# Cross-attention with a merged FFN: two groups of probability products issued as one, the merged weights made a turn later, and a new timetable

## What is computed

```python
x = x + attention(layernorm(x), ctx)      # 16 heads of 16, softmax over 512 keys
x = x + ffn(layernorm(x), W1, b1, W2, b2) # row g has its own W1[g], W2[g]

# attention
qh = heads(q @ Wq.T + bq) / 4;  kh = heads(k @ Wk.T + bk);  vh = heads(v @ Wv.T + bv)
attn = softmax(qh @ kh.T);      out = merge(attn @ vh) @ Wo.T + bo
# ffn: no nonlinearity between the two products
h1 = x @ W1[g].T + b1[g];       h2 = h1 @ W2[g].T + b2[g]
```

## Time and profile before

| | us |
|---|---|
| median of 3 runs | 609.21 (607.52 to 611.81) |
| the profiled execution's own time | 607.91 |
| its span, first to last instruction | 606.1 |
| first `exp` | 40.2 |
| eight turns, first `exp` to the last one's end | 542.5 |
| tail behind the last `exp` | 23.3 |

### The profile page before, as it was taken

One profiled execution on the slowest core, in us unless ns is written; L12 is line 12 of the kernel. 1 busy time (PEld: TensorE's weight loads), 2 busy tenths in 40 slices (PEclk: granted clock), 3 DMA queues, 4 the chain that ended last, 5 costly groups with the idle time before them and its releaser, 6 DMA issues.

```text
span 606.1 us, 13508 instructions
## 1 busy us (share of the span) xinstructions
PE 563.9 (93%) x4353; PEld 342.9 (57%) x4353; DVE 457.4 (75%) x841; ACT 392.5 (65%) x703; POOL 273.5 (45%) x319
## 2 busy tenths in 40 slices
PE   7799999999999999999999999999899989898987
PEld 7545546565665656555655656565555646353667
DVE  6897896889678876888778876888778976883024
ACT  4225776777667676767767676777768665766541
POOL 5260466046832496046832487046831193017311
PEclk9957999999999999999999999999999999995999
DMA  6684343565444733464344723465434523420201
GB/s 208 130 221 158 87 112 84 134 194 132 105 115 118 227 85 94 136 185 135 105 99 130 226 76 100 119 184 152 105 90 106 159 49 96 129 84 6 86 0 36
DMA packets 46704, 72.67 MB, mean 120 GB/s; under 512 B 12162, under 2 KB 22730, under 8 KB 46666
## 3 DMA queue, kind: packets, MB, share of 16 engines
q1 hardware_dynamic: 46666, 72.18, 43.0%
HBM read 41.99 MB, written 4.47 MB: 77 GB/s over the span
## 4 chain that ended last, share of the span: by engine, by line
PE 65%; DVE 16%; issue 9%; ACT 5%; POOL 2%; DMA 2%; DVEq 1%; SPq 0%; ACTq 0%; POOLq 0%
PE pv L535 16%; PE st L521 13%; PE nat L510 10%; PE misc L709 9%; PE misc L595 7%; DVE neg_max L1040 5%; PE misc L585 3%; DVE stats L1051 3%; ACT probs L878 2%; DVE lo L1062 2%; ACT normed L926 2%; DVE y L1119 2%; POOL norm_in L1277 1%; PE st L501 1%; DVE normedT_lo L1068 1%
## 5 line engine op out<-in xcount | busy, mean ns | idle before, releaser
L1040 DVE TENSOR_REDUCE neg_max<-nat 128x1 f32<-128x512 f32 x504 | 336.9, 683 | 99.3 <-PE nat L510 94.9
L878 ACT ACTIVATE probs<-st 128x512 f32<-128x512 f32 x502 | 293.1, 599 | 147.3 <-PE st L521 136.0
L521 PE MATMUL st<-qs,ks 64*128 64x512 f32 x502 | 229.0, 472 | 14.9 <-ACT probs L878 14.3
L510 PE MATMUL nat<-ks,qs 63*128 63x512 f32 x504 | 236.0, 488 | 5.1 <-DVE neg_max L1040 2.4
L521 PEld LDWEIGHTS st<-qs,ks 64*128 64x128 f32 x502 | 92.9, 190 | 127.9 <-ACT probs L878 114.8
L535 PE MATMUL pv<-probs,vs 128*32 128x512 f32 x1024 | 140.2, 620 | 1.2 <-ACT probs L878 1.2
L510 PEld LDWEIGHTS nat<-ks,qs 63*128 63x128 f32 x504 | 92.8, 189 | 32.0 <-DVE neg_max L1040 26.7
L709 PE MATMUL misc<-w_in 64*128 64x256 f32 x512 | 70.7, 378 | 8.3 <-DVE y L1128 8.3
L709 PEld LDWEIGHTS misc<-w_in 64*128 64x128 f32 x512 | 51.4, 186 | 16.0 <-issue 11.0
L1298 POOL TENSOR_TENSOR pair_ctx<-pair_ctx,inv_sum 128x512 f32<-128x512 f32 x15 | 19.1, 1271 | 89.0 <-DMA inv_sum<-inv_dram 89.0
L535 PEld LDWEIGHTS pv<-probs,vs 128*32 128x32 f32 x1024 | 20.3, 108 | 37.4 <-issue 27.9
(11 more groups left out here) (204 smaller groups left out, 1005.9 us busy)
## 6 DMA issues: line engine op xcount, KB each, us to landing
ks<-hi SPq DMA_DIRECT2D x64, 128.0 KB, 2.4
qs<-hi SPq DMA_DIRECT2D x64, 128.0 KB, 2.5
w_in<-w SPq DMA_DIRECT2D x16, 512.0 KB
w_in<-w2T SPq DMA_DIRECT2D x16, 512.0 KB
x_in<-x SPq DMA_DIRECT2D x8, 512.0 KB, 3.4
ctx_in<-ctxT SPq DMA_DIRECT2D x8, 512.0 KB, 3.6
ks<-lo SPq DMA_DIRECT2D x32, 128.0 KB, 2.4
qs<-lo SPq DMA_DIRECT2D x32, 128.0 KB, 2.5
```

The costliest lines, as they stand in the source:

```text
L510: mm((nat_of(n) if bank is None else bank)[:, :], qs[own, 2 * g + jj, c * P:(c + 1) * P], ks[own, 2 * g + jj, :], start=True, stop=True).t ...
L521: mm(st_of(u, prep)[:, :], ks[rows(jp), 2 * g + jj, kc * P:(kc + 1) * P], qs[rows(jp), 2 * g + jj, :], start=True, stop=True).then_inc(st_ ...
L878: act.activation(probs[kc % 2][:, j, :], st_of(u, prep)[:, :], ACT.Exp).then_inc(exp_done, 1)
L1040: dve.tensor_reduce(neg_max[:, g % 2, at:at + 1], (nat_of(n) if bank is None else bank)[:, :], AX.X, ALU.max, negate=True).then_inc(max_do ...
```

## The change

Three things are changed, and the tables of units are all written anew.

1. **`pv` in pairs.** At units with u % 8 = 1, two `pv` are issued one behind the other, 8 products instead of 4. `probs` has four buffers instead of two, and `exp` of a group waits for the `pv` of four groups ago.
2. **W21 of row b-1 is made in turn b**, in units 34 to 47 on the banks 1 and 2, instead of W21 of row b in units 51 to 63. `yT` follows in units 50 to 52 (38 and 39 before), `z` in units 55 to 64, of which the last step falls into the next turn, and the second `out_half` into unit 1 of the next turn. Turn 0 makes no W21. The last turn makes two: that of row 6 in units 10 to 18, its own in units 50 to 63.
3. **SP's and POOL's orders** are changed to fit: the load of the FFN weights and `load_y` come a turn later with respect to their row, `store_out` moves to the beginning of the next turn, and POOL's `b2_parts` moves to the beginning of the turn.

The core of the diff (of the tables only a few lines):

```diff
-CHAIN_UNITS = tuple((4 * k + 2, 4 * k + 2, 4 * k + 3, 4 * k + 3, 4 * k + 4, 4 * k + 4) for k in range(LINKS + 1))
-YT_UNITS = (38, 38, 38, 38, 39, 39, 39, 39)
-Z_UNITS = (44, 44, 45, 45, 47, 47, 48, 49)
-W21_UNITS = (51, 52, 52, 54, 54, 55, 56, 56, 58, 59, 60, 60, 62, 62, 63, 63)
-ATTN_AT = (50, 16)
-NORM_AT = 33
-OUT_AT = (50, 51)
+CHAIN_UNITS = ((3, 3, 3, 3, 4, 4), (5, 6, 6, 7, 7, 7), (10, 11, 11, 12, 13, 13), (14, 15, 15, 16, 16, 16), (19, 19, 19, 20, 21, 21), (22, 22, 22, 23, 23, 24), (26, 27, 27, 27, 28, 28), (29, 30, 30, 31, 31, 32), (34, 35, 35, 36, 36, 37))
+YT_UNITS = (50, 50, 50, 50, 51, 51, 51, 52)
+Z_UNITS = (55, 55, 56, 58, 60, 62, 63, 64)
+W21_UNITS = (34, 35, 36, 37, 37, 38, 38, 40, 41, 42, 43, 43, 45, 45, 46, 47)
+EARLY_W21_UNITS = (10, 11, 11, 11, 11, 11, 12, 13, 14, 15, 16, 16, 18, 18, 18, 18)
+ATTN_AT = (57, 17)
+NORM_AT = 39
+OUT_AT = (63, 65)
...
-Y_AT = (25, 29)
-V_AT = (33, 37)
+Y_AT = (25, 33)
+V_AT = (31, 37)
...
-        probs = [sb(f"probs{i}", [P, 4, S]) for i in range(2)]
+        probs = [sb(f"probs{i}", [P, 4, S]) for i in range(4)]
...
-            def turn(b, post, prep, load):
+            def turn(b, late, post, prep, load):
                 for u in range(UNITS):
                     st(b, u, prep)
                     for row, n in nats_of(b, u, post, prep):
                         nat(row, n)
-                    if u % 4 == PV_AT:
-                        if u > 4:
-                            pv(b, u // 4 - 1)
-                        elif post:
-                            pv(b - 1, 15)
-                    jobs(b, u, post, prep)
+                    if u % 8 == PV_AT:
+                        for n in (u // 4 - 2, u // 4 - 1):
+                            if n >= 0:
+                                pv(b, n)
+                            elif post:
+                                pv(b - 1, 16 + n)
+                    if not prep and u == UNITS - 2:
+                        pv(b, 14)
+                    jobs(b, u, late, post, prep)
...
                 if j == 0:
-                    wait(act, pv_done, 16 * b + kc - 1)
-                act.activation(probs[kc % 2][:, j, :], st_of(u, prep)[:, :], ACT.Exp).then_inc(exp_done, 1)
+                    wait(act, pv_done, 16 * b + kc - 3)
+                act.activation(probs[kc % 4][:, j, :], st_of(u, prep)[:, :], ACT.Exp).then_inc(exp_done, 1)
```

More of the change, by code:

```diff
@@ L617, in link_product, with link_begin @@
                     wo_product(i, t, 2 * n + e)
-            def link_begin(b, k, post, prep):
+            def link_begin(b, k, late, post, prep):
                 if prep:
@@ L733, in jobs @@
+            def jobs(b, u, late, post, prep):
+                for n, at in enumerate(Z_UNITS):
+                    if late and at == UNITS + u:
+                        if n == 0:
+                            z_begin(b - 2, True)
+                        z_step(b - 2, n)
                 for t, at in enumerate(MAXT_UNITS[1]):
@@ L735, in jobs @@
                         if t == 0:
-                            wait(pe, w21_ready, b)
-                            wait_apart(pe, max_done, UNITS * b + 32)
+                            maxT_begin(b, 1, late, post, prep)
                         maxT_half(b, 1, t)
+                for n, at in enumerate(EARLY_W21_UNITS):
+                    if not prep and at == u:
+                        if n == 0:
+                            w21_begin(b - 1, prep)
+                        w21_step(b - 1, n, W21_BANKS, True)
                 for k in range(LINKS + 1):
@@ L781, in jobs, with turn @@
                         if t == 0:
-                            wait(pe, v_ready, 2 * (b + 1) + 1)
-                            if post:
-                                wait(pe, out_ready, 2 * b)
-                            wait_apart(pe, max_done, UNITS * (b + 1) + 16)
+                            maxT_begin(b + 1, 0, post, post, prep)
                         maxT_half(b + 1, 0, t)
-            def turn(b, post, prep, load):
+                for n, at in enumerate(Z_UNITS if prep else LAST_Z_UNITS):
+                    if post and at == u:
+                        if n == 0:
+                            z_begin(b - 1, prep)
+                        z_step(b - 1, n)
+                for n, at in enumerate(LAST_W21_UNITS):
+                    if not prep and at == u:
+                        if n == 0:
+                            last_w21_begin()
+                        w21_step(b, n, LAST_W21_BANKS, False)
+            def turn(b, late, post, prep, load):
                 for u in range(UNITS):
@@ L1135, in turn @@
                         row_max(row, n)
+                    if late and u + UNITS in OUT_AT:
+                        half = OUT_AT.index(u + UNITS)
+                        out_half(b - 2, half, Z_BANKS[half])
                     if load:
```

282 lines of the change are left out of this document (165 added, 117 removed).

## The result

| | before | after |
|---|---|---|
| median us | 610.51 (4 runs beside the changed kernel) | 590.64 (583.31 to 597.14, 4 runs) |
| ratio | | 0.9636, 95% interval 0.9529 to 0.9742 |
| the profiled execution's own time, us | 607.91 | 583.31 |
| tail behind the last `exp`, us | 23.3 | 24.3 |

The change takes 3.6% off by the ratio, 19.9 us by the medians; 590.5 was predicted. The profiled execution of the changed kernel is its fastest, and the four differ with their mean granted clock (0.958 at 583.3 us, 0.945 at 589.9, 0.941 at 591.4, 0.931 at 597.1). That spread turns out to be part of the answer.

What follows compares the result with a forecast made beforehand. DVE was taken to bound units 0-47 of a turn and PE units 48-63, plus three waits. Six turns at -3.1 us, turn 0 -3.1 and the last +3.2 gave -18.5 from 607.9; median 590.5, range 577 to 610.

Steps and rivals of the forecast that it cites:

- The price of a pair: In a pv pair, the second group adds its 0.86 us streaming alone; a pair takes 2.06 us on PE.
- rival C: The second group of a pair pays the 0.34 us change too: -0.4 us a turn, 607 us; chance 0.06.
- The holes: First half, DVE idle behind pv: open holes fall from 4.2 to 3.4 us a turn, -0.8.
- The other term of the first half: First half, DVE work moved away (W21 rests, a y half, an aggregate) against halves added: -1.2 us a turn.
- The waits of the first half: New waits at units 17 (1.0 us, bounds 0 and 3.5), 21 (0.5) and 31 (0.25): +1.7 a turn.
- rival D: Softmax sums come late through SP, holding DVE at unit 8 and ACT at unit 17: 620.7 us; chance 0.10.
- The second half: Units 32-63: work stays 32.8 us, three old waits go (3.4), new ones add 0.6: -2.8 a turn, bounds 0 and -3.4.
- the three waits: Second half before: ACT for the layernorm scale, units 34-37 (1.7 us), late z (0.4), W21's first step (1.3); all go.
- The ends: Turn 0 gains 3.1 us, the last turn loses 3.2, prologue and tail don't change.
- rival E: Half clock in turn 0 and at one more place of the last turn: +6 us in all, 596 us; chance 0.10.
- A: None of the new waits (2.3 us a turn) comes, both banks of nat absorb them: 577 us; chance 0.15.
- B: DVE starves in the pairs, four holes of 1.62 us stay open: +3.1 a turn, 609 us; chance 0.12.

Runs made afterwards that it cites:

- e7: The changed kernel with SP's stacking, gathering, output stores and load ahead of the save, and DVE's odd-pair inverse at unit 7, join at 8: 575.92 us, 0.9437.
- e9: e7 with the first half of y and its statistics at unit 27 instead of 25: 586.32 us, 0.9563.
- e8: The changed kernel measured again, nothing altered: 593.52 us, 0.9673 of the kernel before.
- e6: The changed kernel with normalise at unit 37 instead of 39: 594.91 us, 0.9722 of the kernel before.
- e2: The kernel before with pv in pairs and four probs buffers alone, old timetable: 627.62 us, 1.0269.

## Why the prediction was right, step by step

**The price of a pair: right.** The second group adds its streaming alone: x16 takes 1.93 us where x8 took 1.07, +0.86 as written. Unit 17 with the pair and unit 18 with nothing but `st` and `nat` take 2.18 + 0.34 = 2.52 us; less 2 x 0.23 that is 2.06, the number of the prediction. That refutes rival C. The Trainium skill (TensorEngine Tiling (Array Packing), Key Properties) has the drain at a change of the tiling mode, not of the tile; the trace agrees, and these rows show now what no row of before could, two groups on one change.

**The holes: right in kind, the gain written too small.** A hole that stays open behind a pair is 1.6 us long, as written (1.61 and 1.59 us before the maxima at 277.21 and 293.05 us of turn 3). The prediction had 4.2 us of open holes in the first half and expected 3.4. The idle time before the row maxima in turn 3, units 0 to 31 and 32 to 63, before and then after:

```profile
L1040 DVE TENSOR_REDUCE neg_max<-nat 128x1 f32<-128x512 f32 x32 | 21.4, 680 | 4.1 <-PE nat L510 3.8
```

```profile
L1040 DVE TENSOR_REDUCE neg_max<-nat 128x1 f32<-128x512 f32 x33 | 22.2, 685 | 8.9 <-PE nat L510 8.7
```

```profile
L1101 DVE TENSOR_REDUCE neg_max<-nat 128x1 f32<-128x512 f32 x32 | 21.1, 684 | 1.8 <-PE nat L528 1.2
```

```profile
L1101 DVE TENSOR_REDUCE neg_max<-nat 128x1 f32<-128x512 f32 x32 | 21.2, 685 | 5.3 <-PE nat L528 5.2
```

4.1 became 1.8 (0.7 in e7), not 3.4. In the changed kernel some of DVE's idle time only stands elsewhere, 2.3 us before `lo`, behind the wait at unit 17: DVE idles 4.8 of the 33.5 us, against 3.5 before. In e7, without that wait, it idles 1.6 in all, and that is the gain. The holes were counted as time that only the work written behind the pair can fill; that the two banks of `nat` and the maxima still queued fill some of them too is the likely reason, and was not tested. e9 shows that the placed work is needed all the same, at its full price. The other term of the first half, 1.2 us less work for DVE, is not in the trace: DVE is busy 28.73 us where it was 28.70. The output half written for unit 63 is done only behind the turn's end (at 297.31 us), and so adds its 0.68 us to the next first half.

**The waits of the first half: the right place, the wrong size.** This is the step that failed. The prediction took 1.0 us for ACT at unit 17 with bounds 0 and 3.5, and it was 3.12 in turn 3, 2.8 on the average of turns 2 to 5. It also counted no half clock in this place; the clock falls behind the wait in these turns, which costs some 1.2 us more (the estimate at e8). ACT came at 15.8 us into the turn (16 was written). The division was done at 18.9 (17.3 was written): 0.7 us of the difference is a later save, the rest lies between the save and the division. The spread was issued 3.25 us behind the save, where 2.5 lay between them before, and the chain of waits has the transfer itself with 4.24 us:

```profile
244.42 4.24 DMA inv_sum<-inv_dram
```

From the spread's issue to the start of the division pass 4.39 us here, 3.81 before and 3.87 in e7. The transfer runs while the DMA engines are busy 0.68 of the time, against 0.46 and 0.45 there; that this slows it was not tested. Half of rival D thus came true: the sums did not hold DVE at unit 8 (units 8 to 15 take 7.0 us on the average of the steady turns, 7.9 before), but the divisor held ACT at unit 17. Of the small ones, unit 21 cost nearly what was written: unit 22 takes 1.41 us in e7 for three chain steps, `st` and `nat`, 0.94, so 0.47 against 0.5. At unit 31 DVE waits 0.23 us before the v half, where 0.25 was written.

**The second half: right, by other means in one point.** 33.5 us predicted, 32.2 measured. Two of the three waits went (3.0 us); `z`'s 0.4 stayed, in units where DVE has hardly a gap. The first of them did not go because `normalise` moved (e6), but because the units between it and the aggregate last longer, probably by their W21 steps; in e2, with W21 at its old place, it is there again. The two small waits that were added are there, 0.27 us for ACT's copy of W21 (0.45 written) and 0.38 for the output half (0.15 written). Units 32 to 47 take 17.5 us, as counted (17.4). What is missing from 33.5 lies in units 48 to 63: 14.8 us where 15.4 and 0.6 were written. The terms of those 15.4 add up to 15.9 and were lowered for overlap without a row; 0.7 us of DVE's work there falls behind the turn's end. What makes the rest was not tested.

**Turn 3 as a whole:** 65.4 predicted, 65.7 measured, since +1.6 in the first half and -1.3 in the second cancel. That the sum fits is luck. With the wait out of the way, e7 has 64.0, with a fall of the clock in units 55 to 57, and 62.6 in its turn 2, without one.

**The ends.** Turn 0 gave 5.7 us, not 3.1: its last 16 units gave 3.4, as written, and its first 32 another 2.4 that were not counted. The last turn gave 0.1 and did not lose 3.2. Its W21 of row 6 cost what was written and more (units 8 to 23: 19.7 us against 14.9, +4.8, written +3.2), and the units with `z` came dearer (units 40 to 47 13.1 against 9.8). That was paid back in units 24 to 39 (14.2 against 19.1) and 48 to 63 (13.5 against 16.6). The tail, which was to stay, grew by 1.0 us. Before, the last turn had 17.1 us at half clock from 546.6 us on the earlier trace rows; now it has 3.4 and 6.8 us. Units 32 to 39 alone went from 11.6 to 7.6 us, with 9.8 us of them at half clock before and 1.0 now: so the last turn's gain is probably the clock's. That was not tested by itself.

**The clock: rival E came beside the forecast, not in its place.** The sum was made against the profiled execution: -18.5 us was written and -24.6 came. The median is 7.3 us above that execution, where in the kernel before it was 1.3 with its first three executions and 2.6 with the four beside the changed kernel. Twice (1 - mean granted clock) times the span gives the time at half clock: 49 us in the execution of 583.3 us, 65, 70 and 82 in those of 589.9, 591.4 and 597.1. So 33 us more at half clock go with 13.8 us more time, and the 7.3 us of the median with 16 to 21 (an estimate; only the first of the four has a trace). Turn 0 at half clock for 17 us, 7.5 us in e8, is of that size. So the number 590.5 is right by luck in part, as the sum of two errors that cancel: the profiled execution gained 6 us more than written (3.3 of them in the last turn, where the clock may have a share), and the clock, which rival E priced at +6 with a chance of 0.10 on its own, took 7 in the median.

**The rivals in all.** A: e7 is near what A described, without the wait at unit 17, and has 576 us where A said 577; its terms are not A's, since it has falls of the clock as well. B: did not happen, since its work was there in time; e9 shows its price. C: refuted. D: one of its two waits. E: above.

## What to carry to other kernels

Two long operations of one engine that are bundled save only the change of form, here 0.34 us, unless the engine behind them is given as much work as the hole is long: pairs cost 14 us in the old order, most of it in turns with the clock at half, and were worth 22 and 40 in two timetables that were written for them. Before an inverse, a scale or any small result that goes round over memory is moved, count when its consumer's queue reaches it, and put its issue ahead of bulk stores; two numbers and one queue order gave back 18 us here. Judge the halves of such a change together, and look at every place where an isolated half meets a unit number that was written for the other.
